# A local-attention kernel on one Trainium2 core: half a projection issued before a product, gated products earlier, a turn one step earlier

## What is computed

```python
def attn_layer(x, Wqkv, qs, ksc, Wo):          # 16 heads of 64, windows of 32
    q, k, v = heads(split(x @ Wqkv, 3))
    q = l2norm(q) * qs
    k = l2norm(k) * ksc
    q = q * cos * scale + rotate_half(q) * sin * scale
    k = k * cos / scale + rotate_half(k) * sin / scale
    return merge(local_attention(q, k, v)) @ Wo  # own window and the one before

def ffn_layer(x, g, bln, W1, b1, W2, b2):
    xn = (x - mean) / sqrt(var + 1e-05) * g + bln
    a, gate = split(xn @ W1 + b1, 2)
    return a * gelu(gate) @ W2 + b2

for i in range(6):
    x = attn_layer(shift_tokens(x), ...) + x
    x = ffn_layer(shift_tokens(x), ...) + x
```

## Time and profile before

| | us |
|---|---|
| median of three runs | 3400.34 (3400.24 to 3401.74) |
| the profiled execution | 3401.79 |
| its span, first to last instruction | 3400.0 |
| TensorE busy | 3276.1 (96%) |
| VectorE busy | 2734.4 (80%) |
| GpSimd busy | 2560.1 (75%) |
| ScalarE busy | 2226.2 (65%) |

### The profile page before, as it was taken

The page is one execution under the profiler, slowest core; times in us unless marked ns, Lnnn a source line. Parts: engine busy times, 40 slices in busy tenths (PEclk is TensorE's granted clock), DMA queues, the critical chain, the costliest instruction groups (busy, mean ns, idle before and its releaser), DMA issues. The chain is left out here.

```text
span 3400.0 us, 101399 instructions
## 1 busy us (share of the span) xinstructions
PE 3276.1 (96%) x42193; PEld 2159.4 (64%) x42193; DVE 2734.4 (80%) x3698; ACT 2226.2 (65%) x4397; POOL 2560.1 (75%) x2957
## 2 busy tenths in 40 slices
PE   8999699999999999999999999999999999999996
PEld 5555366666666666666666666666666666666664
DVE  2333598888988888888888888888888888988884
ACT  2222367777677676776776767767767667676774
POOL 0000498888888888888888888888888888888882
PEclk9999899999999999999999999999999999999999
DMA  2000001000001000001000010000010000000000
GB/s 73 1 1 1 4 11 36 11 11 8 11 17 36 8 11 11 11 17 34 11 11 8 11 42 11 8 11 11 11 41 9 11 11 8 16 13 18 11 11 13
DMA packets 62284, 52.53 MB, mean 15 GB/s; under 512 B 11526, under 2 KB 59396, under 8 KB 61828
## 3 DMA queue, kind: packets, MB, share of 16 engines
q1 hardware_dynamic: 61828, 46.05, 5.3%
HBM read 43.93 MB, written 2.10 MB: 14 GB/s over the span
## 5 line engine op out<-in xcount | busy, mean ns | idle before, releaser
L477 POOL TENSOR_TENSOR cosp<-cosp,sinp 128x1024 f32<-128x1024 f32 x384 | 905.7, 2370 | 33.9 <-DVE sinp L976 30.4
L584 PE MATMUL ps<-w_qk,xs 128*128 128x512 f32 x1536 | 748.1, 610 | 11.5 <-ACT sq L792 7.9
L688 PEld LDWEIGHTS ps<-px,w_vo 128*128 128x128 f32 x6144 | 702.5, 192 | 54.2 <-ACT px L833 33.6
L467 POOL TENSOR_TENSOR cosp<-cosp,rr 128x1024 f32<-128x1024 f32 x384 | 722.6, 1903 | 11.4
L688 PE MATMUL ps<-px,w_vo 128*128 128x128 f32 x6144 | 721.3, 276 | 1.9 <-ACT px L833 1.7
L973 DVE TENSOR_TENSOR cosp<-ps,tab 128x1024 f32<-128x1024 f32 x384 | 470.1, 1224 | 262.2 <-PE ps L584 255.8
L792 ACT ACTIVATE sq<-ps 128x1024 f32<-128x1024 f32 x384 | 392.9, 1023 | 344.3 <-DVE sinp L976 344.3
L737 PE MATMUL ps<-pT,xtm 32*128 32x512 f32 x3072 | 467.7, 624 | 34.3 <-DVE hh L1002 19.7
L584 PEld LDWEIGHTS ps<-w_qk,xs 128*128 128x128 f32 x1536 | 263.0, 191 | 343.6 <-issue 343.6
L976 DVE TENSOR_TENSOR sinp<-ps,tab 128x1024 f32<-128x1024 f32 x384 | 466.2, 1214 | 0.0
L982 DVE TENSOR_REDUCE ss<-sq 128x16 f32<-128x1024 f32 x384 | 455.5, 1186 | 3.1 <-POOL rr L452 1.8
(11 more groups left out here) (110 smaller groups left out, 4750.8 us busy)
## 6 DMA issues: line engine op xcount, KB each, us to landing
tab<-in_tab SPq DMA_DIRECT2D x96, 128.0 KB, 2.1
qks<-in_scales SPq DMA_DIRECT2D x96, 128.0 KB, 3.5
w_qk<-in_L_ffn_Wqkv SPq DMA_DIRECT2D x12, 512.0 KB, 6.1
w_v<-in_wv_t SPq DMA_DIRECT2D x6, 512.0 KB, 7.8
w_o<-in_L_ffn_Wo SPq DMA_DIRECT2D x6, 512.0 KB, 8.2
x<-in_L_attn_x SPq DMA_DIRECT2D x16, 128.0 KB, 5.3
out<-w_v SPq DMA_DIRECT2D x16, 128.0 KB, 2.5
w<-in_L_ffn_W SPq DMA_DIRECT2D x6, 341.0 KB
```

The lines of the kernel that those rows point to most:

```text
L467: eng.tensor_tensor(v, v, rr[:, B % 2, HEADS * i:HEADS * i + HEADS].unsqueeze(2).to_broadcast([P, HEADS, DH]), ALU.mult).then_inc(rot_read ...
L477: eng.tensor_tensor(cosp[:, A % 2, i, :], cosp[:, A % 2, i, :], sinp[:, i, :], ALU.add).then_inc(rot_added, 1)
L584: t = eng.matmul(ps[:, u, :], xs[:, n % ROUND, :], w_qk[:, n // TILES % 2, i, 512 * u:512 * u + 512], start=True, stop=True)
L688: t = eng.matmul(Y, w_vo[:, E // TILES % 2, i // HP, i % HP, :], px[:, i, :], start=i == 0, stop=i == HEADS - 1)
```

## The change

It does four things.

1. The projection of q is split. Its first matmul (bank 0) is issued one step earlier, by the new `project_start(A + 1)`, between L724 and L737; the second matmul stays at the head of the next step. The waits that guarded the pair move with the first half.
2. On VectorE the gated products are put elsewhere in the queue: the first of the value step ahead of the turn to `pT`, the one of the rows step right behind that turn and ahead of `statistics`, the last right behind it too.
3. The middle gated product uses bank G(0) in place of G(1).
4. The normalised rows are turned in the value step, behind the gated matmuls, and not in the output step. On ScalarE the normalisation (L802) moves ahead of the square of q, and the affine part (L808) ahead of the square of k, both in the value step.

```diff
-        VALUES = ((11, 0, 2), (12, 1, 1), (12, 2, 2))
+        VALUES = ((11, 0, 2), (12, 1, 0), (12, 2, 2))
...
             def project(n, i):
-                if n % TILES == 0:
-                    eng.wait_ge((wq_in, wk_in)[i], 16 * (n // TILES + 1))
-                for u in range(2):
+                if n % TILES == 0 and i == 1:
+                    eng.wait_ge(wk_in, 16 * (n // TILES + 1))
+                for u in range(i == 0, 2):
                     t = eng.matmul(ps[:, u, :], xs[:, n % ROUND, :], w_qk[:, n // TILES % 2, i, 512 * u:512 * u + 512], start=True, stop=True)
                 t.then_inc((q_done, k_done)[i], 1)
+
+            def project_start(n):
+                if n % TILES == 0:
+                    eng.wait_ge(wq_in, 16 * (n // TILES + 1))
+                eng.wait_ge(xs_ready, 2 * (n + 1))
+                after(eng, k_roped, 2 * n)
+                after(eng, sq_done, 2 * n)
+                eng.matmul(ps[:, 0, :], xs[:, n % ROUND, :], w_qk[:, n // TILES % 2, 0, 0:512], start=True, stop=True)
...
             def step(s):
                 A, B, C, E = s, s - 1, s - 2, s - 3
                 if tile(A):
-                    eng.wait_ge(xs_ready, 2 * (A + 1))
-                    after(eng, k_roped, 2 * A)
-                    after(eng, sq_done, 2 * A)
                     project(A, 0)
...
                     t.then_inc(sims_done, 1)
+                if tile(A + 1):
+                    project_start(A + 1)
...
+            project_start(0)
             for s in range(LAST):
```

VectorE's part (2):

```diff
+                T11, T12 = turn_of(s, 11), turn_of(s, 12)
+                if T12 is not None:
+                    gated(T12, *VALUES[1][1:])
                 if tile(C):
                     eng.wait_ge(weighed, C + 1)
                     after(eng, px_done, 4 * C)
                     eng.transpose(pT[:, :], pn[:, :]).then_inc(p_turned, 1)
+                if T11 is not None:
+                    gated(T11, *VALUES[0][1:])
+                if T12 is not None:
+                    gated(T12, *VALUES[2][1:])
                 T7, T13 = turn_of(s, 7), turn_of(s, 13)
                 if T7 is not None:
                     statistics(T7)
                 if T13 is not None:
                     update(T13)
-                for lag, m, k in VALUES:
-                    T = turn_of(s, lag)
-                    if T is not None:
-                        gated(T, m, k)
```

More of the change, by code:

```diff
@@ L605, in ffn @@
                     t.then_inc(rows_done, 1)
-                T = turn_of(s, 9)
-                if T is not None:
[L608 to L612, removed]
                 T = turn_of(s, 10)
@@ L626, in ffn @@
                         eng.matmul(G(k)[0:fn], w_1[:, f0:f0 + fn], xf[:, :], start=True, stop=True).then_inc(a_done, 1)
+                T = turn_of(s, 8)
+                if T is not None:
+                    eng.wait_ge(xn_ready, TB * (T + 1))
+                    evacuated(s, 1)
+                    for i in range(TB):
+                        t = eng.transpose(G(1)[:, P * i:P * i + P], xn[:, i, :], ident[:, :])
+                    t.then_inc(cols_done, 1)
                 T = turn_of(s, 13)
@@ L794, in ffn @@
             def ffn(s):
[L795 to L808, removed]
                 T = turn_of(s, 10)
@@ L844, in step @@
                     eng.copy(w_vo[:, L % 2, :, 2 * part:2 * part + 2, :], ps[:, 5:7, 0:2 * D].rearrange("p x (i d) -> p x i d", d=D)).then_inc(vo_evac, 1)
+                T = turn_of(s, 8)
+                if T is not None:
+                    eng.wait_ge(shift_done, T + 1)
+                    eng.wait_ge(rows_evac, T + 1)
+                    after(eng, cols_done, T)
+                    for i in range(TB):
+                        at = 2 * HEADS + i
+                        eng.activation(xn[:, i, :], xr[:, i, :], ACT.Identity, bias=shift[:, i:i + 1], scale=rr[:, 1, at:at + 1]).then_inc(xn_ready, 1)
                 if tile(A):
@@ L881, in step @@
                     gelu(T, 0)
+                T = turn_of(s, 8)
+                if T is not None:
+                    eng.wait_ge(ln_in, 32 * (T // NC + 1))
+                    eng.wait_ge(cols_done, T + 1)
+                    after(eng, a_done, 3 * T)
+                    eng.activation(xf[:, :], G(1), ACT.Identity, bias=vec[:, 1:2], scale=vec[:, 0:1]).then_inc(affine_done, 1)
                 if tile(A):
```

## The result

| | us |
|---|---|
| median of four runs after | 3568.14 (3564.82 to 3570.22) |
| median of four runs before | 3400.64 (3400.24 to 3401.74) |
| ratio | 1.049 (95% interval 1.0475 to 1.0506) |
| span of the profiled execution | 3565.0 (3400.0 before) |

The change makes the kernel 4.9% slower, 165 us of span; 156 were forecast. The page of the kernel after, part 1: the number of instructions is the same, TensorE's modelled busy time grows by 58 us and its share falls.

A forecast was written before the change was run, and what follows sets the result against it. TensorE, 96% busy, was taken as the bound, with ScalarE's copying chain ending within 0.06 us of it. +3.59 a round times 45 gave 162; minus 8, plus 5, minus 3 made +156 on 3400.0: 3556 us, own range 3480 to 3595.

The forecast's parts named there:

- the price of the array change: TensorE, each change between full and divided array: about 0.10 us, so the split adds 0.20 us per step.
- The lower bound, no price: TensorE: the added pair of array changes costs 0 instead of 0.20 us per step, making the sum 36 us less.
- The copying chain: ScalarE's three px copies beside TensorE: 3.80 us from L737's start to L688, against 3.86 for TensorE's own chain.
- The 3.80 from L737 to L688: Copying chain's length: 2.08 to ScalarE's first bank, 1.56 for three copies, 0.16 for release and weight load.
- Net 0: Rows step: L737's stall of 1.69 goes, but GpSimd's rotation holds the turn of q; 0 us per round.
- a rows step of 15.48 as before: Sign in the profile after: no break in L737, yet the rows step keeps its length of 15.48 us.
- wait for G(0): Value step: TensorE waits 0.99 us for the last bank that ScalarE empties, before the middle gated product.
- wait for the square: Value step: L593 waits 0.5 us for the square of k, which now stands behind `xf` on ScalarE.
- The 3 us taken back at the end: Term of the sum: 3 us subtracted for steps at the end where L737 waits longer.
- slower by less: Rival, chance 0.14: the value step's waits do not bind, the rows step gains 0.4 every round; +77, about 3477 us.
- Slower by more: Rival, chance 0.07: GpSimd's and VectorE's work follows the late square into the output step, delaying its turn of q; 3610 us.
- Faster: Rival, chance 0.10: L688 follows the half projection at once, so the waits won count; -82, about 3318 us.

The follow-up runs named there:

- a quarter of the copies: The changed kernel with the four copies to px cut to 4 of 16 heads from the second tile on; 3451.6 us, 1.014 of the kernel before.
- the gated product ahead, alone: The kernel before with one VectorE edit, the gated product of the rows step put ahead of the statistics; 3393.2 us, ratio 0.997.
- the half ahead of the similarities: The kernel before with only the projection of q split, its first matmul one step earlier, before the similarities; 3648.1 us, one run.
- The split alone: The kernel before with part 1 only, the first matmul of q between the similarities and L737; 3493.5 us, ratio 1.026.

## Why the prediction was right

**Part 1 and the price of the array change.** Forecast +1.00 for the gate step, +0.56 for the output step; the trace has +0.99 and +0.55. L593 takes 1.06 to L744, as worked out from the two kinds of change in the earlier trace rows. The lower bound, no price, is ruled out twice: 0.20 is left in the gate step with a quarter of the copies, and 0.20 goes when the same half stands ahead of the similarities. The Trainium skill ("TensorEngine Tiling (Array Packing)", Key Properties) says that a change of tiling mode drains TensorE. The traces show the cost and not the drain; it is in line with the rule, at about 0.10 us each way.

**The copying chain.** That the half projection no longer covers the copies was the main step. It is shown by removal: with a quarter of the copies the waits go and 0.79 us come back in the gate and in the output step. The Trainium skill ("TensorEngine Tiling (Array Packing)", PSUM Bottleneck) warns that the copy out of PSUM may become the bottleneck once tiling has sped up TensorE. The trace agrees as far as it goes: behind the tiled product of 1.93 us three copies take 1.56 us more. No run here has that product untiled. The 3.80 from L737 to L688 came out as 3.69 with 0.10 lost again inside L688, the same sum for a reason I had not seen.

**The rows step.** "Net 0" is right up to the turn of q: the 0.45 won by L693 is lost there again (0.43). The release by GpSimd's rotation is in the rows, and with the rest of the kernel fixed (the gated product ahead, alone) the earlier product won 3 tenths of a per cent. What I had not worked out is that a second bound, the late start of L688, lies only 0.33 behind. As signs I had named a rows step of 15.48 as before; counted from turn to turn it is 15.04, and the loss stands in the value step.

**The value step.** Forecast: wait for G(0) 0.99, measured 0.98; wait for the square 0.5, measured 0.59; net of rows and value +2.03, measured +2.03 in plain rounds. Both waits are shown by taking each away, 0.57 and 0.86 a step. That the net agrees to the second decimal is luck: single terms are up to 0.11 off and cancel (the four gated passes take 1.79 and not 1.72, L693 comes 3.69 behind L744 and not 3.80).

**What was mis-sized.** In rounds with fused weights rows and value grow by 1.45 (15.04 + 17.80 less 15.48 and 15.90); I had 1.63, some 4 us too much. Gate and output steps came 1 us short of the sum. The 3 us taken back at the end were not there, the tail grew by 4. And the sum had no term for irregular steps, which cost 7 us more than before. So the misses cancel in part: 156 less 5, plus 7, plus 7 is the measured 165. The rival "slower by less" fell with the rows of the two waits. "Slower by more" fell in the output step: its turn of q follows L693 by 3.67 and waits for nothing. "Faster" fell with the copies, and its arithmetic with it: with a quarter of the copies L693 does follow the half projection at once, as that rival asks, and the kernel was still 1.4% slower and not 82 us faster.

## What to carry to other kernels

Filling a stall with work taken from further back is free only if that work was covering nothing where it stood: look for the second chain that ends beside it, here a chain of copies that ended 0.06 us ahead of need. A stall can also be what absorbs irregular stops (below), so what it costs is less than its length. Two edits that each live on the same stall do not add: 89 and 10 us became 168. When a result buffer is swapped, check in which order the buffers come free.

## What was not expected of the hardware

**A group behind a wait can take longer.** From the turn of the tile to the next product are 0.11 us when nothing was waited for the earlier trace rows, and L688's group is 3.57 long; behind a wait the group is 3.67 in every run above, where nothing else holds what follows, and the 0.10 lies between its first two matmuls (0.21 apart, not 0.11). The turn of q takes 0.93 to its successor behind a wait, not 0.88. It is no fixed price of every wait: L593, which waits ahead of a full-array matmul behind divided ones, takes 1.02 and not 1.06.

**The clock after an irregular stop.** TensorE stops now and then for nothing that the trace names. In the changed kernel such a stop of 1.84 us in a rows step was followed by a granted clock at the lower of the two levels (1.2 in place of 2.4 GHz): L744's group took 3.62 us to its successor, not 1.93.

```profile
1654.20 0.34 PE L729 MATMUL ps<-kT,qT 64*32 64x64 f32 x14 [1.84 <-issue]
1654.47 1.13 PE L593 MATMUL ps<-w_qk,xs 128*128 128x512 f32 x2
1655.53 3.69 PE L744 MATMUL ps<-pT,xtm 32*128 32x512 f32 x16
```

The stretches view (us, busy time and instructions of the five engines, then the granted clock, the share of the DMA engines and GB/s):

```profile
1643.00:1655.00 12.00, 10.16 (x185) 7.91 (x184) 10.72 (x19) 7.87 (x12) 10.93 (x8) 1.00 0.08 21
1655.00:1658.50 3.50, 3.50 (x18) 1.21 (x16) 1.37 (x2) 0.65 (x2) 2.33 (x8) 0.59 0.03 10
```

Four rows steps of the changed kernel have such a pair. Their stops are 1.73 to 1.86 us long and the steps 3.2 to 3.4 us over the typical one; a step with a stop of 1.75 us and no lower clock is 1.67 over. So the lower clock costs about 1.5 to 1.7 us each time. Not every such stop brings it: in the kernel before one of 1.78 us did and one of 1.83 us did not.

The run with the half ahead of the similarities has the lower clock in its first steps too, there with TensorE busy for 99.7 of 120 us and a mean of 0.89. The split alone is busy for 111.2 us of the same stretch, at 1.00.

```profile
430.00:550.00 120.00, 99.68 (x1389) 65.23 (x1388) 85.75 (x96) 63.88 (x117) 91.96 (x105) 0.89 0.04 11
```

**A stall that absorbed stops.** The rows steps of the changed kernel add up to 24 us over their typical length, those of the kernel before to 8. The kernel before, with a stop of 1.83 us at the same place:

```profile
1780.19 0.35 PE L724 MATMUL ps<-kT,qT 64*32 64x64 f32 x16 [1.83 <-issue]
1780.46 2.00 PE L737 MATMUL ps<-pT,xtm 32*128 32x512 f32 x16
```

L737 does not break off there, because the gated product is done by the time TensorE comes to it, and the step is only 0.26 longer than typical. The stop took the place of the stall. In the kernel before six rows steps have stops of over 0.3 us without a lower clock, 5.8 us in all, and are 0.5 over typical together; in the changed kernel six such steps have 8.2 us of stops and are 7.7 over. The rest of the difference are the steps with the lower clock: four, 13 us over typical, before two with 4. Why the stops happen, and why some bring the lower clock, no run here settles.
